# A selective scan with experts: the slot list inverted on the chip, rows gathered per block, experts from tile 3

## The reference

```
delta = softplus(xn @ W_delta.T + bias)              # per token and feature
B_t, C_t = xn @ W_B.T, xn @ W_C.T                    # 256 features x 16 states
h = exp(delta*A) * h + (exp(delta*A) - 1)/A * B_t * x_t     # over 2048 tokens in order
y_t = sum over the 16 states of h * C_t

scores = xn @ Wr + br                # 8 experts, the best 2 of each token, softmax of the two
expert(e) = gelu(xn @ W1[e] + b1[e]) @ W2[e] + b2[e]         # 256 -> 1024 -> 256
out = sum of the two weighted experts
```

## Time and profile before

| | |
|---|---|
| median of three runs | 1290.01 us |
| profiled execution | 1290.72 us, span 1289.0 us |
| PE busy | 1174.5 us (91%) |
| DVE busy | 977.8 us (76%) |
| POOL busy | 835.1 us (65%) |
| ACT busy | 803.8 us (62%) |
| DMA | 186.96 MB, mean 145 GB/s |

### The profile page before, as it was taken

How to read it: one execution, slowest core, us unless ns; L and a number is a source line. 1 busy time by engine, 2 the same in 40 slices (tenths; PEclk the granted TensorE clock), 3 DMA queues, 4 the chain that set the end, 5 groups by cost and what they waited for, 6 DMA issues and landing times.

```text
span 1289.0 us, 22376 instructions
## 1 busy us (share of the span) xinstructions
PE 1174.5 (91%) x7674; PEld 730.4 (57%) x7674; DVE 977.8 (76%) x1362; ACT 803.8 (62%) x1341; POOL 835.1 (65%) x733
## 2 busy tenths in 40 slices
PE   1467887789899999999999999999999999999996
PEld 0342333455556666666666666666666666666652
DVE  6767998887777777777776866767777776776788
ACT  3553445577788775666567567576756657566631
POOL 2536788357878676665766676666675766667662
PEclk9998989999999999999999999999999999999998
DMA  9942234667768753445344354344444354334423
GB/s 295 301 126 103 80 107 141 229 209 233 260 210 270 235 139 111 119 102 141 104 111 131 93 138 131 90 121 134 105 124 122 100 136 119 107 114 105 103 62 138
DMA packets 87387, 186.96 MB, mean 145 GB/s; under 512 B 12784, under 2 KB 64880, under 8 KB 77168
## 3 DMA queue, kind: packets, MB, share of 16 engines
q1 hardware_dynamic: 59280, 152.80, 35.3%
q0 software_dynamic: 18000, 22.42, 10.6%
q10 hardware_dynamic: 10000, 10.38, 3.3%
HBM read 135.48 MB, written 57.96 MB: 150 GB/s over the span
## 4 chain that ended last, share of the span: by engine, by line
PE 72%; POOL 6%; DVE 6%; issue 5%; ACT 2%; DMA 1%; DVEq 0%; SPq 0%; POOLq 0%; ACTq 0%
PE bank L1165 39%; PE bank L1214 15%; PE bank L1227 15%; POOL xs L953 3%; DVE hb L1069 3%; POOL ax L938 2%; PE bank L1194 1%; PE bank L1239 1%; DVE bank L1047 1%; POOL whl L948 1%; DMA wst<-in_W 1%; DVE bank L1081 1%; PE bank L1246 1%; DVE ysum L1090 1%; DVE bank L1043 0%
## 5 line engine op out<-in xcount | busy, mean ns | idle before, releaser
L938 POOL TENSOR_TENSOR ax<-ax,x 128x512 f32<-128x512 f32 x214 | 272.1, 1279 | 287.2 <-ACT ax L843 285.2
L1165 PE MATMUL bank<-k_xT,k_WB 128*128 128x512 f16 x1536 | 379.5, 384 | 47.2 <-DVE hb L1069 34.4
L1165 PE MATMUL bank<-k_xT,k_WC 128*128 128x512 f16 x1536 | 377.0, 382 | 0.8 <-DVE ysum L1090 0.8
L1047 DVE TENSOR_TENSOR bank<-ax,bank 128x512 f32<-128x512 f32 x214 | 148.4, 693 | 222.9 <-PE bank L1165 197.9
L1165 PEld LDWEIGHTS bank<-k_xT,k_WB 128*128 128x128 f16 x1536 | 146.2, 99 | 200.8 <-DVE hb L1069 51.2
L1165 PEld LDWEIGHTS bank<-k_xT,k_WC 128*128 128x128 f16 x1536 | 151.4, 99 | 186.3 <-issue 7.2
L1069 DVE TENSOR_TENSOR_SCAN hb<-aexp,state,bank 128x512 f32<-128x512 f32 x192 | 244.4, 1273 | 0.0
L833 ACT ACTIVATE aexp<-k_dcur,k_A 128x512 f32<-128x512 f32 x256 | 180.8, 711 | 72.1 <-DVE hb L1069 66.8
L1214 PE MATMUL bank<-xbt,k_x 128*128 128x256 f16 x1872 | 218.7, 274 | 3.8 <-ACT k_x L881 3.8
L1214 PEld LDWEIGHTS bank<-xbt,k_x 128*128 128x128 f16 x1872 | 183.8, 98 | 42.9 <-ACT k_x L881 4.8
L1081 DVE SCALAR_TENSOR_TENSOR bank<-hb,k_rA,bank 128x512 f32<-128x512 f32 x240 | 179.9, 749 | 1.8
(11 more groups left out here) (144 smaller groups left out, 1321.6 us busy)
## 6 DMA issues: line engine op xcount, KB each, us to landing
k_x<-wsplit SPq DMA_DIRECT2D x78, 1024.0 KB, 4.8
wst<-in_W SPq DMA_DIRECT2D x32, 512.0 KB, 5.8
wsplit<-whl SPq DMA_DIRECT2D x32, 512.0 KB, 5.6
xs<-zero ACTq DMA_DIRECT2D x1, 10140.0 KB, 61.1
xb<-xs SPq DMA_DIRECT2D x39, 260.0 KB, 4.5
b<-in_b SPq DMA_DIRECT2D x39, 128.0 KB
k_x<-in_x SPq DMA_DIRECT2D x4, 1024.0 KB, 9.7
stB<-in_WBT SPq DMA_DIRECT2D x8, 512.0 KB, 10.0
```

Source lines behind the costliest of these rows:

```text
L938: nc.gpsimd.tensor_tensor(ax[:, k % MR], ax[:, k % MR], x32[:], ALU.mult).then_inc(ax_done, 1)
L1047: v.tensor_tensor(bank, ax[:, RANK[g] % MR], bank, ALU.mult).then_inc(ux_done, 1)
L1165: ins = mm(bank[:], W[:, a, kc, n, hf * P:(hf + 1) * P], xT[:, c, b, kc, :], start=(k == 1), stop=(k == 3 * KC))
```

## The change

Nothing is scattered and no memory is zeroed. The prologue writes all 4096 rows in token order to `xrows`, with a row of zeros in the middle (HOLE = 2048). It then inverts the slot list. A slot number is split into two digits, slot = 128*hi + lo. VectorE makes for both choices masks of hi (32 x 78 per partition) and lo (32 x 128); the hi masks are multiplied by the token's number, one by GpSimd, one by ScalarE; and 64 matmuls of TensorE add up, for each of the 9984 slots, the number of the token that has it. Empty slots get the row of zeros. Eight small operations of VectorE turn this into `row`, `second` and `target` for all blocks at once. GpSimd gathers each block's rows with two indirect DMAs. The first four pieces of weights are split in the prologue.

Experts begin at tile 3, blocks are of seven tiles (first eight) and six. DIRECT tiles are the odd ones below 59 in place of 84. To make room, the rings shrink: AR from 5 to 4, MR from 4 to 3.

```diff
-E0 = 36
-EARLY, LONG, STEP = E, 6, 5
+E0 = 3
+EARLY, LONG, STEP = E, 7, 6
...
-        allowed = always + ([spare] if g < E0 - 2 or g >= E_END else [])
+        allowed = always + ([spare] if g >= E_END else [])
...
-    AR, MR, HR = 5, 4, 3
+    AR, MR, HR = 4, 3, 3
     LEAD = AR - 1
...
-        act.dma_start(io["xs"].rearrange("(p r) d -> p r d", p=P),
-                      zero[:].unsqueeze(1).broadcast_to([P, NSLOT // P, D + META])).then_inc(keep["zeros_out"], 16)
...
+        sp.wait_ge(meta_set, 1)
+        sp.dma_start(io["xrows"][0:HOLE, :].rearrange("(i p) d -> p i d", p=P),
+                     xall[:, 0:NT // 2, :]).then_inc(keep["rows_out"], 16)
+        sp.dma_start(io["xrows"][HOLE + 1:T + 1, :].rearrange("(i p) d -> p i d", p=P),
+                     xall[:, NT // 2:NT, :]).then_inc(keep["rows_out"], 16)
+        for k in range(AHEAD):
+            store_piece(sp, io, keep, k)
+            load_piece(sp, io, keep, k + W_BUF)
...
+        for i in range(NT):
+            ins = nc.scalar.activation(hot_hi[1][:, i], hot_hi[1][:, i], ACT.Copy, scale=tid[:, i:i + 1])
...
+        ch.run(v.tensor_scalar(slot_hi[:], slotf[:], 1.0 / P, -(P / 2 - 0.5) / P, ALU.mult, ALU.add))
+        ch.run(v.tensor_scalar(slot_hi[:], slot_hi[:], ROUND, -ROUND, ALU.add, ALU.add))
+        ch.run(v.scalar_tensor_tensor(slot_lo[:], slot_hi[:], -float(P), slotf[:], ALU.mult, ALU.add))
+        for k in range(2):
+            v.tensor_tensor(hot_hi[k], slot_hi[:, k].unsqueeze(2).broadcast_to([P, NT, NS]),
+                            lane[:, 0:NS].unsqueeze(1).broadcast_to([P, NT, NS]), ALU.is_equal).then_inc(hi_made, 1)
+        for k in range(2):
+            for h in range(2):
+                half = slice(h * NT // 2, (h + 1) * NT // 2)
+                v.tensor_tensor(hot_lo[k][:, half], slot_lo[:, k, half].unsqueeze(2).broadcast_to([P, NT // 2, P]),
+                                lane[:].unsqueeze(1).broadcast_to([P, NT // 2, P]), ALU.is_equal).then_inc(lo_made, 1)
...
+        for k in range(2):
+            pe.wait_ge(hi_named[k], 1)
+            for i in range(NT):
+                if i % (NT // 2) == 0:
+                    pe.wait_ge(lo_made, k * 2 + i // (NT // 2) + 1)
+                ins = mm(banks[5][:, k * NS:(k + 1) * NS], hot_lo[k][:, i], hot_hi[k][:, i],
+                         start=(i == 0), stop=(i == NT - 1))
...
-        def scatter(j):
...
+        def gather(b):
+            if b >= 2:
+                pool.wait_ge(turn_made, USE["turn", b - 2] + 1)
+                pool.wait_ge(w_set, b - 1)
+            for s in range(BS):
+                at = b * BS + s
+                nc.gpsimd.indirect_dma_start(
+                    out=xb32[:, b % 2, s], out_offset=None, in_=io["xrows"],
+                    in_offset=bass.IndirectOffsetOnAxis(keep["row"][:, at:at + 1], 0)).then_inc(xb_in[b % 2], 16)
...
+        pool.wait_ge(keep["rows_out"], 3 * 16)
+        gather(0)
         for g in range(TILE_N):
...
+            for b in range(NBLK):
+                if block_start(b) + 2 == g:
+                    slot_data(b)
+                if block_start(b) + 3 == g and b + 2 < NBLK:
+                    gather(b + 2)
```

More of the change, by code:

```diff
@@ L54 @@
 NPIECE = 4
-META = 4
+META = 2
+NS = NSLOT // P
+ROUND = float(3 << 22)
+HOLE = T // 2
 class Chain:
@@ new lines, with quiet @@
+TURN_AT = {block_start(b) - 2: b for b in range(NBLK)}
+TAKE_Y_AT = {block_start(b + 1) + 5 + (b + 1 < EARLY): b for b in range(NBLK)}
+DIRECT = set(range(1, block_start(EARLY), 2))
+SPLIT_TILES = [g for g in range(TILE_N) if g not in DIRECT]
+RANK = {g: i for i, g in enumerate(SPLIT_TILES)}
+def quiet(g):
+    while any(k in TURN_AT for k in (g - 1, g, g + 1)):
+        g += 1
+    return g
+Z_AT = {quiet(c * TILES + 13 + 15 * hf): (c + 1, hf) for c in range(NCH - 1) for hf in range(KC)}
+ROW_AT = {quiet(c * TILES + 21 + 16 * hf): (c, hf) for c in range(NCH) for hf in range(KC) if (c, hf) < (NCH - 1, 1)}
@@ new lines, in turn_bank_uses, with tile_banks @@
+def turn_bank_uses():
+    order = []
+    for g in range(TILE_N):
+        if g in ROW_AT:
+            order.append(("row",) + ROW_AT[g])
+        if g in Z_AT:
+            order.append(("z",) + Z_AT[g])
+        if g in TURN_AT:
+            order.append(("turn", TURN_AT[g]))
+    return {name: i for i, name in enumerate(order)}
+def tile_banks(always, spare):
+    last, bank, before = {}, [], []
+    for g in range(TILE_N):
+        allowed = always + ([spare] if g >= E_END else [])
+        pick = min(allowed, key=lambda k: last.get(k, -1))
+        bank.append(pick)
+        before.append(last.get(pick))
+        last[pick] = g
+    return bank, before
@@ new lines, in split_order, with pieces_before, row_add_step @@
+def split_order():
+    order = [(0, 0), (0, 1), (1, 0), (1, 1)]
+    for e in range(E):
+        order += [(e, 2), (e, 3)]
+        if e + 2 < E:
+            order += [(e + 2, 0), (e + 2, 1)]
+    return order
+PIECES = split_order()
+AHEAD = 4
+PIECE_AT = {k: block_start((k - AHEAD) // 4) + 3 + k % 4 for k in range(AHEAD, SPLITS)}
+def pieces_before(expert, last_part):
+    n = PIECES.index((expert, last_part)) + 1
+    return [(n + HL_BUF - 1 - r) // HL_BUF for r in range(HL_BUF)]
+def row_add_step(c):
+    return (c + 1) * TILES + (20 if c == 0 else 14)
@@ new lines, in adds_before, with load_piece @@
+def adds_before():
+    count, n = {}, 0
+    for g in range(TILE_N + 8):
+        for c in range(NCH - 1):
+            if row_add_step(c) == g:
+                count["row", c] = n
+                n += 1
+        if g - 3 in TAKE_Y_AT:
+            count["block", TAKE_Y_AT[g - 3]] = n
+            n += BS
+    return count, n
+def load_piece(sp, io, keep, k):
+    (ex, pc), r = PIECES[k], k % W_BUF
+    wst = keep["wst"]
+    if k >= W_BUF:
+        sp.wait_ge(keep["p_lo"], k - W_BUF + 1)
+    if pc < KC:
+        sp.dma_start(wst[:, r, :], io["W1"][ex, pc * P:(pc + 1) * P, :]).then_inc(keep["piece_in"][r], 16)
+    else:
+        fc = (pc - KC) * (FC // 2)
+        sp.dma_start(wst[:, r, :].rearrange("p (c d) -> p c d", d=D),
+                     io["W2"][ex, fc * P:(fc + FC // 2) * P, :].rearrange("(c p) d -> p c d", p=P))\
+            .then_inc(keep["piece_in"][r], 16)
@@ L232, in _ @@
                 sp.dma_start(stC[:, par], wc_v[:, :, bass.ds(at, GW)]).then_inc(c_in[par], 16)
+        for k in range(W_BUF):
+            load_piece(sp, io, keep, k)
+        sp.wait_ge(zero_set, 1)
+        sp.dma_start(io["xrows"][HOLE:HOLE + 1, :], zero[:]).then_inc(keep["rows_out"], 16)
+        sp.wait_ge(meta_set, 1)
[6 more added lines that the diff above has]
+            load_piece(sp, io, keep, k + W_BUF)
     @block.gpsimd
@@ L520 @@
[L520 to L535, removed]
@@ L538 @@
[L538 to L552, removed]
@@ L577 @@
[L577 to L602, removed]
@@ L1015, in _ @@
             if g == 0:
-                pool.wait_ge(keep["zeros_out"], 16)
-            for k in range(SPLITS):
+                gather(1)
+            for k in range(AHEAD, SPLITS):
                 if PIECE_AT[k] + 3 == g:
-                    low_piece(k)
-            if g < NT:
-                scatter(2 * g)
-                scatter(2 * g + 1)
+                    low_piece(nc, pool, keep, k)
             b, q = HIDDEN_AT.get(g - 4, (None, None))
```

337 lines of the change are left out of this document (155 added, 182 removed).

## The result

The changed kernel takes 1375.98 us (median of four runs, 1372.09 to 1378.13) against 1290.37 for the kernel before, four runs on the same chip: ratio 1.0652, 95% interval 1.0618 to 1.0687. It is slower by 6.5%. The forecast was slower, at 1326, in a range of 1286 to 1350; the time lies 50 us above the one and 26 above the other. The profiled execution has a span of 1376.4 us.

What follows compares the result with a forecast made beforehand. TensorE was taken to bound the expert stage. Span 1254.7 with experts from tile 3, plus 18.7 prologue, 30.6 rings, 10 clock and 11 seven-tile blocks gave 1325.0 us, 1326 as a median, range 1286 to 1350.

Steps and rivals of the forecast that it cites:

- tail: The tiles after the last expert work: shrinks from 17 to 11 tiles, from 59.5 to 41.4 us.
- Experts from tile 3: Expert stage: 39 blocks over 242 tiles instead of 203 add 103.2 us; with the shorter tail, span 1254.7, a gain of 34.3.
- The shorter rings and the clock: Expert stage from tile 59: late ax behind eleven softplus steps costs 30.6 us in TensorE holes, slow clock after them 10.
- The longer prologue: Before the first scan: masks, namings and list inversion add net 18.7 us, between 12 and 30.
- Rival D: Prologue: the list is inverted too slowly, rows late or masks contending with GpSimd, +10 us, 1336; chance 0.60 together with forecast.
- The seven-tile blocks: First eight blocks: softplus holes and late ax cost about 11 us over before's own stalls, ends -10 and +25.
- Gather for load: Expert stage: 78 gathers come, 64 scatters go; costed at nothing because TensorE bounds and GpSimd is idle a third.
- A: Rival: the rings are deep enough, 1274 us, faster by 1.2%; chance 0.15 with mixtures that end faster.
- C: Rival: ScalarE and GpSimd bound the seven-tile blocks, 34 us a block instead of 32.2, 1340 us; chance 0.09.

Runs made afterwards that it cites:

- run 10: The changed kernel with ScalarE making ax three tiles ahead instead of two, and the down projection in four parts instead of three: 1288.63 us, 0.9973 of the kernel before.
- run 9: The changed kernel, rings kept short, with ScalarE making ax three tiles ahead and, after a block's first tile, saved state, exp and ax before the GELUs: 1312.61 us.
- runs 6 and 7: The changed kernel with rings of five and four and two weight-piece buffers instead of three: 1323.02 us; the same with the down projection in four parts: 1298.20 us.
- run 11: The changed kernel with ax three tiles ahead, the down projection in four parts, and both mask namings on ScalarE, GpSimd idle during the masks: 1289.71 us, 0.9980.
- run 12: The changed kernel with ax three tiles ahead, the down projection in four parts, and each softplus moved to a block's third step: 1278.55 us, 0.9895.

## Why the prediction was wrong

The forecast span was 1325.0; measured 1376.4, 51.4 more. By the forecast's own steps:

| step | forecast | measured | miss |
|---|---|---|---|
| first scan | 127.8 | 136.9 | +9.1 |
| tiles 0 to 3 | 12.2 | 12.7 | +0.5 |
| eight blocks of seven | 8 x 32.2 = 257.6 | 263.2 | +5.6 |
| 31 blocks of six | 1143.6 - 257.6 = 886.0 | 918.8 | +32.8 |
| tail | 41.4 | 44.9 | +3.5 |

*Experts from tile 3: the step that failed.* "TensorE's work in that zone grows by 39 x 2.58 = 100.6 us" priced a tile that is added to a block as matmuls alone. But a block of five had expert work in all of its steps, and the sixth step has none. There nothing hides the loop product, scan, next projection on two banks, and the step costs 3.50 in place of 2.58. The trace of the kernel before had the price, 3.51 us in its six-tile blocks, and the forecast did not look there. Cutting the down projection so that every step has some took 0.92 us off each block without a softplus, and 25.9 us off 59 to 245 (run 10 against 9). The prediction named the sign of this, "a softplus-free block takes over 27 us": it takes 27.39.

*The shorter rings and the clock: mechanism right, size low.* Ring and clock together were 30.6 + 10 = 40.6 us; run 9, which keeps the rings short and has ScalarE fill them earlier, puts them at 918.8 - 867.2 = 51.6. By block against run 9: the seven softplus steps at a block's start cost 3.7 to 6.8, mean 5.4 (forecast 3.2 and 1.1 of clock), the two that stand one step later 5.4 and 5.1, the two that stand two later 1.7 each. That adds up to the 51.6: blocks without a softplus lose nothing, as the forecast said. All nine holes that the forecast named came, 2.69 to 3.50 us, 26.6 together (forecast 28.6). What was low is, first, the clock: eight of them were followed by slow matmuls, 1.5 to 3.0 us each by the start of the work behind, 14.4 in all against 10, and the one at tile 95 was not. Second, two ax come late, not one: ahead of the hole seven of the nine blocks have a smaller one of 0.56 to 0.66 us.
By these two terms and a base of 841.3 (run 10; the forecast's base, with the stalls of the kernel before, was 886.0 - 40.6 = 845.4) the stage is 841.3 + 25.9 + 51.6 = 918.8. The terms are differences of runs 10, 9 and the changed kernel, so they add up by construction; runs 6 and 7 give the same two by another way, 51.3 (918.8 - 867.5) and 23.7. Of the miss of 32.8 in this stage the bare step is 25.9, the rings and the clock 11.0, and the base takes off 4.1.

*The longer prologue.* Rival D's mechanism was at work beside the forecast's, at its price (+10, measured +9.1). VectorE's masks stand against GpSimd's products: 20.3 us in place of 15.4. The work ahead of them ends at 103.83 and not near 100: the product at 99.31 takes 1.96 us where its like at 98.21 took 0.61, and the scaling at 101.75 takes 1.55 where the next of its size takes 0.20, both beside GpSimd's low halves (98.22 to 103.26). Behind the masks it is 5.3 us in place of 4.7. With GpSimd idle the six masks take 14.2 us (run 11, from 102.39 to 116.54), so the price per element was about right.
The Trainium skill (SBUF — State Buffer, "Who interferes with whom") says that a VectorE instruction with two inputs in SBUF contends with a GpSimd instruction that reads there, and calls the port pair that they share "an exclusive lock". The trace agrees as far as it goes: GpSimd's naming lies beside the first pair for 4.3 us, and the pair takes 8.65 - 4.49 = 4.16 more.

*The seven-tile blocks.* Low by 5.6 us (its terms 5 + 1 + 4.4 make 10.4, put at 11). ScalarE waited 26.6 us for stored pieces there, about twice; late ax cost 9.6 (run 9), and with ax on time the places of the softplus cost another 10 (run 12). *Tail:* 41.6 us in run 9, so 3.3 of the 3.5 go with ScalarE's order too. *Gather for load* cost next to nothing: TensorE's weight load waits once, 2.9 us, for gathered rows, and GpSimd twice, 5.3 us.

*The rivals.* None carried it. A held the rings to be deep enough, which they aren't in the order given; as memory they are, from tile 59 on (run 9), and this the prediction did not think of: it took "depth" and "lead" as one thing. C's 34 us a block was 32.9.

## What to carry to other kernels

A tile that is added to a pipelined block costs what its step costs when nothing hides it: look for the step that loses its cover, and take the price from rows where a step has no cover, rather than from the busy time of the engine that bounds; here the kernel before had such rows. When a ring is cut, ask which comes late, the buffer's release or the producer's turn in its own order; here three buffers did all that four did once the producer filled them before its long stops. And of two fixes, the order counts: with ax late, evening out TensorE's steps cost 59 us; with ax on time it gained 25.

## What the runs showed of the hardware

- VectorE's operations take longer while GpSimd works: a pair of 128x2048 masks took 8.65 us beside GpSimd and 4.49 alone, a 128x312 comparison 2.40 and 0.48, a 128x78 scaling 2.01 and 0.20.
- TensorE's clock: behind a hole of 2.85 us two projections took 4.29 us to the start of the next work (granted clock 0.66 over 5 us), behind one of 2.75 us 2.60 (granted clock 1.00). A hole of 2.69 us at 759.53 was followed by 4.29, one of 2.61 by the usual 1.47 for its first projection. The length of the hole alone did not decide it.
- Without the zero fill ScalarE's wait of 4.1 us for C's weights is gone from the waits of the changed kernel; this was not tried by itself.
